# Adding x to the attention rows, and the gated value to the output, with accumulating transfers from GpSimd's queue

## The reference

```
# layer 0: attention over the 64 rows of a sequence, then a normalisation by channel
f   = softmax(phi(ctx) theta(x)^T);   w_y = Wz (f g(x)) + bz
w_y = gamma * (w_y - mean) * rsqrt(var + eps) + beta
z   = w_y + x                                        # input of layer 1
# layer 1: one RWKV block, state taken from ctx
xn  = ln(z);  sx = shift(xn)                         # row before minus row
r, k, v, w, g = projections of xn + sx * (...)       # five mixes
att = scan over 64 steps of  s = k v + w s,  out = r (u k v + s)
x1  = z + (groupnorm(att) * g) Wo^T
xn2 = ln(x1); sx2 = shift(xn2)
rr  = sigmoid(xr ffn_Wr^T);  kk = relu(xk ffn_Wk^T)^2
out = x1 + rr * (kk ffn_Wv^T)
```

## Time and profile before

| | |
|---|---|
| Median of 3 runs | 745.33 us (740.27 to 745.39) |
| Profiled execution | 745.93 us, its span 743.7 us |
| Mean granted TensorE clock | 0.959 of full |
| Attention and `norm_params` | 0 to about 178 us |
| Fill and first pass | about 178 to 282 us |
| Bodies 1 to 6 | about 282 to 651 us, 61.9 us each |
| Last pass and drain | about 651 to 743.7 us |
| Busy | PE 661.4, DVE 633.3, ACT 366.4, POOL 259.9 us |

### The profile page before, as it was taken

One profiled execution on the slowest core, in us unless ns is written; L12 is line 12 of the kernel. 1 busy time (PEld: TensorE's weight loads), 2 busy tenths in 40 slices (PEclk: granted clock), 3 DMA queues, 4 the chain that ended last, 5 costly groups with the idle time before them and its releaser, 6 DMA issues.

```text
span 743.7 us, 9716 instructions
## 1 busy us (share of the span) xinstructions
PE 661.4 (89%) x2736; PEld 358.8 (48%) x2736; DVE 633.3 (85%) x989; ACT 366.4 (49%) x805; POOL 259.9 (35%) x186
## 2 busy tenths in 40 slices
PE   7689999988996869999999899899999989956996
PEld 5466666656442214453444435445344443523574
DVE  2499999994467899999999999999999999879623
ACT  3468888872242327446255444644625544352431
POOL 1850000001003674554536336355453633831000
PEclk9689999999998988999999999999999999986899
DMA  2611211110075146055152523705615232350000
GB/s 63 214 45 57 68 58 56 56 57 29 1 147 107 36 77 142 1 113 132 39 114 64 105 53 60 169 0 113 135 35 113 69 72 59 82 114 0 0 29 28
DMA packets 38298, 54.17 MB, mean 73 GB/s; under 512 B 4626, under 2 KB 21154, under 8 KB 38146
## 3 DMA queue, kind: packets, MB, share of 16 engines
q1 hardware_dynamic: 36866, 50.46, 30.3%
q0 software_dynamic: 1408, 3.43, 1.4%
HBM read 16.13 MB, written 4.19 MB: 27 GB/s over the span
## 4 chain that ended last, share of the span: by engine, by line
PE 28%; DVE 27%; issue 12%; ACT 4%; POOL 1%; DMA 1%; DVEq 1%; SPq 1%; ACTq 0%; POOLq 0%
DVE state L1295 10%; PE ps_a L794 5%; PE ps_a L765 4%; PE ps_c L853 3%; PE ps_c L867 3%; DVE x L1258 2%; DVE state L1282 2%; PE ps_att L833 2%; DVE st L1226 2%; PE ps_a L805 2%; PE ps_a L777 2%; PE ps_c L865 2%; PE ps_a L803 2%; PE ps_c L765 1%; DVE sx L1339 1%
## 5 line engine op out<-in xcount | busy, mean ns | idle before, releaser
L669 POOL TENSOR_TENSOR x<-x,xn 128x1024 f32<-128x1024 f32 x35 | 84.4, 2413 | 201.2 <-DVE x L1258 201.2
L1295 DVE TENSOR_TENSOR_SCAN state<-ps_w,state 128x512 f32<-128x512 f32 x128 | 145.8, 1198 | 0.7
L765 PE MATMUL ps_a<-x,wsq 128*128 128x512 f32 x256 | 117.9, 599 | 5.5 <-ACT xn L1033 3.0
L664 POOL TENSOR_TENSOR state<-vb,k 128x2016 f32<-128x2016 f32 x23 | 107.1, 4655 | 22.8 <-DMA vb<-v 16.0
L1300 DVE TENSOR_TENSOR vb<-state,r 128x2048 f32<-128x2048 f32 x32 | 95.4, 2981 | 1.6
L765 PEld LDWEIGHTS ps_a<-x,wsq 128*128 128x128 f32 x256 | 47.2, 191 | 65.6 <-issue 52.0
L1258 DVE SCALAR_TENSOR_TENSOR x<-ps_a,vec,sx 128x512 f32<-128x512 f32 x80 | 57.3, 742 | 14.2 <-PE ps_a L794 12.9
L794 PE MATMUL ps_a<-mix_t,w 128*128 128x512 f32 x128 | 62.5, 610 | 6.1 <-ACT mix_t L1038 6.1
L296 ACT ACTIVATE probs<-ps_f,negmax 128x256 f32<-128x256 f32 x128 | 58.9, 472 | 2.0 <-DVE negmax L345 1.2
L646 POOL TENSOR_TENSOR rs<-ve,mhalf 128x4 f32<-128x4 f32 x16 | 27.9, 1744 | 82.6 <-DVE ve L1232 82.6
L345 DVE TENSOR_REDUCE negmax<-ps_f 128x2 f32<-128x512 f32 x64 | 41.2, 685 | 7.5 <-PE ps_f L218 5.0
(11 more groups left out here) (170 smaller groups left out, 1258.1 us busy)
## 6 DMA issues: line engine op xcount, KB each, us to landing
vb<-v SPq DMA_DIRECT2D x128, 256.0 KB, 5.8
x<-in_x SPq DMA_DIRECT2D x32, 128.0 KB, 2.1
c<-in_ctx SPq DMA_DIRECT2D x32, 128.0 KB, 2.1
x_chunk<-in_x SPq DMA_DIRECT2D x8, 512.0 KB, 7.4
out<-sx SPq DMA_DIRECT2D x8, 512.0 KB, 3.5
wsq<-in_wsq POOLq DMA_DIRECT2D x1, 1024.0 KB, 5.2
wsq<-in_wsq POOLq DMA_DIRECT2D x1, 768.0 KB, 7.0
s<-in_s POOLq DMA_DIRECT2D x1, 512.0 KB, 7.9
```

Of the source, the lines that this page charges most:

```text
L664: nc.gpsimd.tensor_tensor(st[q][:, :, :, 1:L], src[:, :, :, 0:L - 1], wide(k[p][h][:, :])[:, :, :, 0:L - 1], ALU.mult).then_inc(kv_at(n, h ...
L669: nc.gpsimd.tensor_tensor(x5[j % 2][:, :, :], x5[j % 2][:, :, :], xn[:, :, 1:L1], ALU.add).then_inc(x5_ready, 1)
L765: mm = nc.tensor.matmul(bank[:, :], wsq[:, weight, c, P * o:P * o + P], src(c), start=(c == 0), stop=(c == EC - 1))
L1295: nc.vector.tensor_tensor_scan(row, w[h][:, :], row, 0.0, ALU.mult, ALU.add).then_inc(scanned, 1)
```

## The change

`load_x` goes. For chunks 1 to 7 ACT's `a_bias` computes `wyz * bna + bnb` in place (128 x 1024), and a transfer issued by GpSimd (`z_add`) adds x from HBM to `wyz`. Chunk 0 is as before. `a_bias(n+2)` and `z_add(n+2)` stand near the head of the body. On the output, SP stores x1 from `wyz` as soon as it is there (`store_x1`), and GpSimd issues a transfer that adds `y` to the stored rows in HBM (`add_out`); `c_final` goes. The factor 0.5 is multiplied into ffn_Wv by GpSimd during the attention. `prev0` is loaded at the start of layer 1 instead of with the other weights.

```
-            for w_, at in ((2, 9), (1, 12)):
+            nc.gpsimd.tensor_scalar(t["wsq"][:, FV, :, :], t["wsq"][:, FV, :, :], 0.5, 1.0, ALU.mult, ALU.mult).then_inc(s_pick, 1)
+            for w_, at in ((2, 10), (1, 13)):
...
 # SyncE
-            def load_x(n):
-                wait(sp, z_ready, n)
-                sp.dma_start(xr_in[:, :, :], d["x"][bass.ds(n * TILES, TILES)].rearrange("a p f -> p a f")).then_inc(x_in, 16)
-            def store(n):
-                sp.wait_ge(out_ready, n * 2 + 2)
-                sp.dma_start(out[bass.ds(n * TILES, TILES)].rearrange("a p f -> p a f"), y).then_inc(stored, 16)
+            def store_x1(n):
+                sp.wait_ge(x1_ready, n * 2 + 2)
+                sp.wait_ge(stored, n * 16 + 16)
+                sp.dma_start(out[bass.ds(n * TILES, TILES)].rearrange("a p f -> p a f"), wyz[:, bass.ds(n * TILES, TILES), :]).then_inc(x1_stored, 16)
+            def body(n, c=True, a=True):
                 if a:
                     spread_v(n + 1, 0)
                 if c:
-                    store(n - 1)
+                    store_x1(n - 1)
                 if a:
                     spread_v(n + 1, 1)
...
 # GpSimd
+            def z_add(n):
+                pool.wait_ge(x_biased, n + 1)
+                pool.dma_start(wyz[:, bass.ds(n * TILES, TILES), :], d["x"][bass.ds(n * TILES, TILES)].rearrange("a p f -> p a f"),
+                               accum_op=ALU.add).then_inc(z_ready, 16)
+            def add_out(n):
+                pool.wait_ge(y_mid, n * 2 + 4)
+                pool.wait_ge(x1_stored, n * 16 + 16)
+                pool.dma_start(out[bass.ds(n * TILES, TILES)].rearrange("a p f -> p a f"), y, accum_op=ALU.add).then_inc(stored, 16)
             def body(n, p, z=True):
                 q = 1 - p
                 b_kv(n, p, 0, 1)
+                if z:
+                    z_add(n + 2)
                 prev(n + 1, sx_ready, xprev, t["prev1"], xn)
...
                 b_kv(n + 1, q, 0, 0)
                 add_x(n + 1, 4)
+                add_out(n - 1)
...
 # ScalarE
+                if isinstance(n, int) and n == 0:
+                    act.wait_ge(x_in, 16)
+                    nc.scalar.activation(xr_in[:, :, :], xr_in[:, :, :], ACT.Identity, bias=t["bnb"][:, 0:1]).then_inc(x_biased, 1)
+                else:
+                    wy = wyz[:, bass.ds(n * TILES, TILES), :]
+                    nc.scalar.activation(wy, wy, ACT.Identity, bias=t["bnb"][:, 0:1], scale=t["bna"][:, 0:1]).then_inc(x_biased, 1)
             def body(n, p, z=True):
                 q = 1 - p
+                if z:
+                    a_bias(n + 2)
                 a_w(n, 1)
...
                 a_dec(n + 1)
-                if z:
-                    a_bias(n + 2)
                 a_w(n + 1, 0)
...
 # VectorE: a_z only for chunk 0; a_zm waits for the transfer (z_ready, n * 16)
-            def c_final(n):
-                for i in range(2):
-                    dve.wait_ge(y_mid, n * 2 + i + 3)
-                    nc.vector.scalar_tensor_tensor(y[:, 2 * i:2 * i + 2, :], y[:, 2 * i:2 * i + 2, :], 0.5,
-                                                   wyz[:, bass.ds(n * TILES + 2 * i, 2), :], ALU.mult, ALU.add).then_inc(out_ready, 1)
```

More of the change, by code:

```diff
@@ L32 @@
 L1 = L + 1
-LATE = 32
+LATE = 31
 HH = H // 2
@@ L152, in _ @@
                              (t["dw1"], d["dw1"]), (t["s0"], d["s0"]),
-                             (t["prev1"], d["prev1"]), (t["prev0"], d["prev0"])):
+                             (t["prev1"], d["prev1"])):
                 pool.dma_start(dst[(slice(None),) * len(dst.shape)], src).then_inc(t["s_late"], 16)
@@ L491, in rwkv @@
     xn2_ready, xprev2, sx2_ready, xk_ready, xr_ready = sem("xn2_ready"), sem("xprev2_ready"), sem("sx2_ready"), sem("xk_ready"), sem("xr_ready")
-    relu_ready, kk_ready, rr_ready, y_mid, out_ready, stored = sem("relu_ready"), sem("kk_ready"), sem("rr_ready"), sem("y_mid"), sem("out_ready"), sem("out_stored")
+    relu_ready, kk_ready, rr_ready, y_mid, x1_stored, stored = sem("relu_ready"), sem("kk_ready"), sem("rr_ready"), sem("y_mid"), sem("x1_stored"), sem("prev0_in_and_out_stored")
     c_done = sem("c_matmuls_done")
@@ L626, in body @@
                 if c:
-                    store(n - 1)
+                    store_x1(n - 1)
                 if a:
                     spread_v(n + 1, 1)
-            load_x(1)
             spread_v(0, 0)
@@ L636, in _ @@
                 body(n)
-            body(CHUNKS - 2, x=False)
-            body(CHUNKS - 1, a=False, x=False)
-            store(CHUNKS - 1)
+            body(CHUNKS - 2)
+            body(CHUNKS - 1, a=False)
+            store_x1(CHUNKS - 1)
+            sp.wait_ge(x1_stored, 16 * CHUNKS)
             sp.wait_ge(stored, 16 * CHUNKS + 16)
@@ L715, in drain_pass @@
                 rstd(n - 1, ln2_var, ln2_rstd, ve2, rs2)
+                add_out(n - 1)
+            pool.dma_start(t["prev0"][:, :, :], d["prev0"]).then_inc(stored, 16)
             rstd(0, ln1_var, ln1_rstd, ve1, rs1)
@@ L719, in _ @@
             first_pass(0, 0)
+            pool.wait_ge(stored, 16)
             with pool.Fori(1, CHUNKS - 4, 2) as n:
@@ L1237, in a_z @@
                 z = wyz[:, bass.ds(n * TILES, TILES), :]
-                nc.vector.scalar_tensor_tensor(z, z, t["bna"][:, 0:1], xr_in[:, :, :], ALU.mult, ALU.add).then_inc(z_ready, 1)
+                nc.vector.scalar_tensor_tensor(z, z, t["bna"][:, 0:1], xr_in[:, :, :], ALU.mult, ALU.add).then_inc(z0_ready, 1)
             def a_zm(n):
-                moments(n, z_ready, n + 1, st1b, mv1, ve1, st1, mv1_s, ln1_var)
+                first = isinstance(n, int) and n == 0
+                moments(n, z0_ready if first else z_ready, 1 if first else n * 16, st1b, mv1, ve1, st1, mv1_s, ln1_var)
             def a_shift(n):
@@ L1346, in fill_pass @@
                 a_mod(n + 1, 1)
-                a_z(n + 2)
                 a_mod(n + 1, 2)
@@ L1396, in body @@
                 a_mod(n + 1, 4)
-                c_final(n - 1)
             def last_pass(n, p):
@@ L1426, in _ @@
             dve.sem_inc(y_mid, 2)
-            dve.sem_inc(stored, 16)
             dve.wait_ge(init_done, 3)
```

11 lines of the change are left out of this document (3 added, 8 removed).

## The result

The changed kernel takes 750.22 us (median of 5 runs, 749.41 to 751.2), the kernel before in the same job 743.57 (5 runs, 740.27 to 745.39). The ratio is 1.0095, with a 95% interval of 1.0071 to 1.012: the changed kernel is slower, by about 1%. The forecast was 750.4. The profiled execution took 749.43 with a span of 747.9, against 745.93 and 743.7 before: 3.5 and 4.2 us more.

What follows compares the result with a forecast made beforehand. PE and DVE both looked full, and a body could win at most PE's 3.7 us of waits. Bodies +3.5 and tail +1.6 made +5.1 us: profiled 745.93 becomes 751.0, median 750.4, own range 746 to 756.

Steps and rivals of the forecast that it cites:

- the tail: Last gate to end of span: GpSimd's issue and the adding transfer's landing take 6.1 us instead of 4.55, +1.6.
- a_z: Removed from DVE in bodies 1 to 5: its 1.2 us are lost as L1300 waits for GpSimd's product, 0 a body.
- The first pass and body 1: Before b_att, ACT wins some 0.5 us and DVE none; body 1 then grows by 0.6.
- c_final and the issue: DVE's freed 3.2 us mostly wait for GpSimd's product; issue price c taken as 0.8, gain 0.1, counted as 0.
- Rival A: GpSimd's issues of add_out and z_add delay DVE, deciding from c = 1.6 on: 754, or 763 us; chance 0.17.
- `prev`: On GpSimd behind z_add's issue, a_shift waits for it: about 0.3 us on DVE, inside the room left.
- a_bias: Moved to ACT's body head, 1.13 us: c_gn and the body's end 0.72 late, bodies 1 to 5 +3.5 in all.
- The last pass: GpSimd's product may start 2.5 us sooner but then holds DVE's c_gn: 0, bounds -1.5 and +1.
- The signs: Profile after: body about 62.6 us, PE waits 1.7 for xn and 1.2 for the tanh, DVE busy about 2 less.
- B: DVE bounds: its freed time closes both its gaps on PE, 2.4 us a body, giving 735 us; chance 0.12.
- C: Bodies unchanged, ACT's 1.13 taken up by slack or paid by the first pass: 745 to 747 us; chance 0.18.
- D: Adding transfers work row by row, slowly: a 15 us landing costs +10, over 35 us a_zm waits; chance 0.03.

Runs made afterwards that it cites:

- the z part alone: Kernel before with load_x and a_z of chunks 1 to 7 replaced by a_bias at the body's head and z_add: 746.05 against 744.37 us, ratio 1.0024.
- `a_bias` back: Changed kernel with a_bias of the bodies behind a_dec again and z_add behind add_x(n + 1, 2): 747.32 us against 744.37 before, ratio 1.0053.
- the fastest kernel: The kernel with both edits, with the last chunk's x1 added on DVE and stored plainly by SP: 738.41 us against 742.62 before, ratio 0.994.
- the output part alone: Kernel before with store_x1, add_out and 0.5 in the weight, without c_final, z made as before: 745.34 against 744.37 us, ratio 1.0017.
- the kernel with both edits: Changed kernel with a_bias behind a_dec, z_add behind add_x(2), and GpSimd's product (0, 1) ahead of add_x(4): 740.17 us against 742.62 before, ratio 0.9969.
- a second pass of ACT: Changed kernel with one more 128 x 1024 activation on an unused buffer behind a_bias in the bodies: 753.77 us against 742.62 before, ratio 1.0143.

## Why the prediction was right, and where its terms were off

The total was right to 0.2 us, and part of that is luck. It said +5.1 from one profiled execution to another, and +3.5 came (+4.2 in the span); between the medians it was +6.65, from a median of before that is 1.8 lower with the two runs added to the three that I had. So the rise was 1.55 too small and the base 1.8 too high. Within the span two terms cancel: bodies 1 to 5 came to +2.6 where +3.5 was said, and the tail to +2.6 where +1.6 was said.

**a_z: right.** L1322 of part (1, 1) starts at 456.10 and ends at 460.90, 4.80 long instead of 3.68. From the mark it starts 0.8 us earlier and ends 0.35 later, by as much as GpSimd's product (454.26 in this trace, 4.49 long) starts later. So the cover that was named held: nothing of the 1.2 us arrives behind it.

**The first pass and body 1.** `a_norm` ends just before `b_att`, as was said against the earlier trace rows:

```profile
278.74 2.08 ACT L1041 ACTIVATE zn<-wyz,rs 128x256 f32<-128x256 f32 x4 [8.50 <-POOL rs L644]
280.72 0.57 ACT L1093 ACTIVATE attc<-ps_att 128x512 f32<-128x512 f32 x1
```

I had ACT 0.5 early here, and body 1 at +0.6. The pass gained 0.06 and body 1 lost 1.07, together +1.0. It isn't shown to be the price of `a_bias`: with the z part alone, which has `a_bias` in the same place, the two stages take 163.63 us, 0.2 more than before. I can't divide this further: first pass and body 1 together go from 163.45 to 164.80 over the ten profiles, and a stretch of lower granted clock lies at about 272 to 296 us (mean 0.79 before and after, 0.72 with `a_bias` back, 0.82 in the fastest kernel).

**c_final and the issue: the mechanism right, the price near.** The 3.2 us did come to no more than the room before GpSimd's product. The issue record is 1.33 us long, and GpSimd's next instruction starts 0.87 after its start, inside it. I had the product at 4.48, and behind the issue it took 4.98; so the issue cost 1.4 rather than 0.8, as much as its record is long, and in place of a gain of 0.1 came a loss, 0.2 a body with the output part alone. In the changed kernel it lies under ACT's delay. Rival A was nearer than it looked: the prediction has A decide from a c of 1.6 on, but its own sum (0.8 us too late at 2.2) gives 1.4, which is what was measured. It still didn't decide, since DVE was late by 0.2 us only, and the 0.3 put down for `prev` never showed.

**a_bias: right in place and sign, almost twice too large.** This is the step that was mis-sized: 0.72 us a body, measured 0.38. `c_gn` is late by about as much as said, 0.8: 405.12 to 416.96 are 11.84 us from the mark, before they were 11.03. The sentence "From `c_gn` DVE works without a break to `c_shift`" didn't hold for before. There `a_mod(0)`, the third pair from `c_gn` on, came at 418.04 and took 1.61 us; in after the same pair (419.61) takes 1.41, and the one ahead of it ends at its start. That slack took 0.3 of the 0.8. At the scan behind it 0.48 is left, at `c_shift` 0.45, at the body's end 0.38. I had looked for idle time between instructions alone, and not at a pair that was longer than its like. The lower bound of 0.4, that only part of the delay reaches `c_key`, is where the value lies.

**The tail: too small by 1.0.** +1.6 was forecast, +2.59 came, within -1 and +4.5. 6 us was taken for issue to end, 6.85 measured, and the issue came 0.29 behind the gate where 0.1 was taken. The 3.2 us for a plain transfer, set beside the sum, would have made the tail shorter by 1.2; it is longer.

**The last pass: 0 forecast, -0.5 measured**, inside its bounds. GpSimd's product, which answers to the earlier trace rows, waits 7.19 us there instead of 9.31, and starts 1.6 us sooner from the mark:

```profile
662.64 4.88 POOL L660 TENSOR_TENSOR state<-vb,k 128x2016 f32<-128x2016 f32 x1 [7.19 <-DMA vb<-v]
```

That is hardly the cause. With the z part alone the product waits 9.29 us, as before, and the stretch from the last body's mark to the next is 0.9 us shorter than before; with the output part alone it waits 7.02, and the stretch is 0.1 shorter. What differs is the granted clock in this stretch (third from the end), 0.75 before and 0.82 after, then with the z part alone:

```profile
651.48:700.14 48.66, 34.10 (x109) 17.68 (x108) 41.44 (x42) 19.49 (x33) 7.82 (x6) 0.75 0.21 41
653.60:701.72 48.12, 32.67 (x109) 16.61 (x108) 41.92 (x40) 19.60 (x33) 7.96 (x4) 0.82 0.20 47
652.84:700.64 47.80, 32.57 (x109) 16.62 (x108) 41.39 (x42) 19.48 (x32) 7.83 (x6) 0.82 0.21 42
```

The higher clock goes with the 0.5 us; no run took this stage apart, so the cause stays open.

**The signs.** The body (62.2 against 62.6), the wait for `xn`, DVE's wait of 0.5 for the root and L1322 at 5.70, ending with GpSimd's product plus 2.2, came as said. The wait for the tanh was 0.8 and not 1.2, and the one before `a_mix` kept 0.5. DVE's busy time was to fall by 2 us a body and didn't fall: the hold that the prediction itself names fills it.

Of the rivals, A and B each hold a true mechanism. B's was that DVE's freed time could close gaps on PE. It does so only when both conditions against it are taken away, GpSimd's product beside L1322 and ACT's pass at the head, and then 0.74 us of the 2.4 come (the kernel with both edits). C is refuted by the z part alone, whose bodies are as long as those of after. D is refuted by the landings: 7.1 and 9.7 us among others, 6.85 at the end.

**What stays open.** The medians differ by 6.65 us, the profiled spans by 4.2. In the ten profiles layer 1 starts between 173.9 and 180.0 us, for kernels whose attention hardly differs, so this stage scatters more than the change moves. Whether the change lengthens it by a little, a single profile for each kernel can't tell. The two parts timed alone are not separable from no change (1.0024 and 1.0017), and the changed kernel's 1.0095 comes from only 5 runs of each.

## What to carry to other kernels

Taking work off a busy engine pays only if the engine isn't then held at the next place: look at the instruction behind the freed gap and ask what another engine will be doing beside it. Two chains that arrive nearly together have to be shortened together; here one edit gave 0.2 us, the other nothing, and the two 1.12. An adding transfer in place of an instruction costs its landing where nothing stands behind it, so the last piece is better finished on the engine and stored plainly.

## What the runs showed of the hardware

- A transfer of 512 KB added to HBM from GpSimd's queue took 6.85 us from issue to the end of the span, at a quiet moment; the plain stores of that size in the kernel before landed in 3.5 (median). Over the whole kernel, most of them among other transfers, the adding ones had a median of 9.7 into HBM and 7.1 into SBUF; the plain stores of x1 beside them had 7.4, so the step from 3.5 to 9.7 isn't all the price of adding.
- DVE's product of two SBUF operands (2.29 us alone) took 3.45 to 7.97 when GpSimd was in its own product at its start, and in each case it ended 2.2 us behind GpSimd. DVE's scans with one operand in PSUM kept their 4.55 us beside the same GpSimd work. The Trainium skill (SBUF — State Buffer, Who interferes with whom) has it that a VectorE instruction with two SBUF inputs contends with a GpSimd instruction that reads SBUF, that the port pair they share is an exclusive lock, and that the order of issue decides who blocks. The rows agree: DVE's product always came second, and the 2.2 us behind GpSimd's end are the whole of its own time.
- GpSimd's product took 4.49 us at other places, 4.98 right behind one issue of 512 rows and 5.83 behind four. With the start of that product 0.87 and 2.28 us behind that of the issue, the issue's price is 1.36 and 3.62 us, which is the length of its record (1.33 and 3.62), though the next instruction starts before the record ends.
- In bodies 2 to 5 of after, with a wait of 1.7 us in each, PE's granted clock had a mean of 1.00. In the run with a second pass of ACT the wait was 2.8 us, and behind it the clock fell to 0.53 for 2 us and 0.62 for 2 more, that is for most of the time to 1.2 GHz from 2.4, in body 3. Body 4 had a mean of 0.85 over 10 us at the same place, body 2 stayed at 1.00 in every slice behind the same wait, and 5 as well. Where it fell, a body was 0.8 us longer.
